# Twelve early tiles read two a batch, bias and tables moved, and a reordered drain in an attention and mixture-of-experts kernel

## The reference

```python
mod = (_silu(c) @ wmod).reshape(32, 6, 1, -1)
sa, ca, ga, sb, cb, gb = mod[:, 0] ... mod[:, 5]     # ga, gb: magnitude at least 0.25
h = _layernorm(x) * (1 + ca) + sa
...
x_proj = (h @ w_in.T + b_in).reshape(b, l, 16, -1); q, k, v = split(x_proj, 3)
att = softmax(einsum('blhd,bmhd->blmh', q, k) / sqrt(8), axis=2)
x = x + ga * (einsum('blmh,blhd->blhd', att, v).reshape(b, l, d) @ w_out.T + b_out)
h = _layernorm(x) * (1 + cb) + sb
...
logits = h @ router_w; assignments = argmax(logits); weights = softmax(logits)[assignments]
hid = gelu(einsum('nd,edf->nef', h, w1) + b1)        # 14 experts, 256 hidden
all_out = einsum('nef,efd->ned', hid, w2) + b2
x = x + gb * all_out[assignments] * weights
```

## Time and profile before

| | us |
|---|---|
| median of 3 runs | 638.29 (637.71 to 638.56) |
| the profiled execution's own time | 640.0 |
| its span on the core | 638.2 |
| busy: DVE | 557.4 (87%) |
| busy: ACT | 541.7 (85%) |
| busy: PE | 476.2 (75%) |
| busy: POOL | 476.6 (75%) |

### The profile page before, as it was taken

The page is one execution under the profiler, slowest core; times in us unless marked ns, Lnnn a source line. Parts: engine busy times, 40 slices in busy tenths (PEclk is TensorE's granted clock), DMA queues, the critical chain, the costliest instruction groups (busy, mean ns, idle before and its releaser), DMA issues.

```text
span 638.2 us, 11779 instructions
## 1 busy us (share of the span) xinstructions
PE 476.2 (75%) x2518; PEld 266.5 (42%) x2518; DVE 557.4 (87%) x1420; ACT 541.7 (85%) x2306; POOL 476.6 (75%) x661
## 2 busy tenths in 40 slices
PE   5446878877877877887878888876876679888870
PEld 3112334433333433343434333332432369778760
DVE  6977999999999999999999999997988768778770
ACT  1588999999999999999999999998999637666640
POOL 4453766888888888888887888867767857777774
PEclk9999965567566566556565565565555559999995
DMA  6355554545455555555454545556655124676740
GB/s 190 107 151 143 145 145 136 149 141 150 136 148 151 149 149 148 141 157 155 141 160 132 140 141 159 134 139 167 165 167 158 49 75 125 195 194 193 196 121 4
DMA packets 75416, 91.65 MB, mean 144 GB/s; under 512 B 12910, under 2 KB 59028, under 8 KB 75344
## 3 DMA queue, kind: packets, MB, share of 16 engines
q1 hardware_dynamic: 66810, 72.93, 42.4%
q0 software_dynamic: 6560, 16.83, 7.1%
q10 hardware_dynamic: 1976, 1.15, 0.7%
HBM read 58.41 MB, written 33.29 MB: 144 GB/s over the span
## 4 chain that ended last, share of the span: by engine, by line
ACT 42%; DVE 15%; DMA 10%; PE 8%; issue 8%; POOL 8%; SPq 8%; POOLq 0%; DVEq 0%; ACTq 0%
ACT scores L765 41%; DVE neg_max L1149 6%; SPq L481 6%; DMA x_s<-table 3%; DMA parts_dram<-parts 3%; DMA out_dram<-out_room,ids_s 2%; PE scores L1027 2%; POOL out_dram L743 2%; PE scores L1036 2%; POOL table L691 1%; DVE bn L1083 1%; POOL rstd L630 1%; SPq L557 1%; DMA out_dram<-out_room,x_s 1%; PE side_a L917 1%
## 5 line engine op out<-in xcount | busy, mean ns | idle before, releaser
L765 ACT ACTIVATE scores<-scores,neg_max 128x256 f32<-128x256 f32 x1024 | 466.1, 781 | 21.6 <-DVE neg_max L1149 21.2
L765 ACT ACTIVATION_READ_ACCUMULATOR scores<-scores,neg_max 128x1 f32 x1024 | 378.0, 542 | 0.0
L1149 DVE TENSOR_REDUCE neg_max<-scores 128x4 f32<-128x1024 f32 x256 | 308.9, 1210 | 5.8 <-PE scores L889 4.8
L889 PE MATMUL scores<-k_stack,q_stack 64*128 64x256 bf16 x1024 | 148.8, 391 | 83.0 <-ACT scores L765 72.2
L889 PEld LDWEIGHTS scores<-k_stack,q_stack 64*128 64x128 bf16 x1024 | 34.6, 106 | 168.4 <-ACT scores L765 122.4
L691 POOL DMA_INDIRECT table<-rows,place_i x64 | 65.8, 1028 | 30.3 <-issue 29.5
L743 POOL DMA_INDIRECT out_dram<-out_room,ids_s x61 | 62.3, 1022 | 18.6 <-issue 14.9
L799 ACT ACTIVATE hid<-scores,w_e 128x128 f32<-128x128 f32 x154 | 48.1, 364 | 15.8 <-PE scores L1027 15.4
L917 PE MATMUL side_a<-w_gated,opt_t 128*128 128x128 f32 x128 | 50.6, 499 | 0.0
L1027 PE MATMUL scores<-x_t,w_e 128*128 128x128 f32 x308 | 49.8, 286 | 0.1
L629 POOL TENSOR_TENSOR rstd<-mv,eps_s 128x4 f32<-128x4 f32 x37 | 7.4, 200 | 56.9 <-DVE mv L1114 41.4
(11 more groups left out here) (172 smaller groups left out, 874.6 us busy)
## 6 DMA issues: line engine op xcount, KB each, us to landing
x_s<-table SPq DMA_DIRECT2D x77, 192.5 KB, 2.6
q_stack<-parts_dram SPq DMA_DIRECT2D x192, 64.0 KB, 2.5
parts_dram<-parts SPq DMA_DIRECT2D x31, 384.0 KB, 2.7
k_stack<-parts_dram SPq DMA_DIRECT2D x186, 64.0 KB, 2.3
mod_b<-mod_rows SPq DMA_DIRECT2D x32, 256.0 KB, 3.8
x_s<-in_x_dram SPq DMA_DIRECT2D x13, 256.0 KB, 3.6
w1x_s<-in_w1x_dram SPq DMA_DIRECT2D x7, 258.0 KB, 2.9
w_s<-in_w_dram SPq DMA_DIRECT2D x7, 256.0 KB, 3.1
```

Of the source, the lines that this page charges most:

```text
L765: last = act.activation(buf[:, k * L:k * L + L], buf[:, k * L:k * L + L], ACT.Exp, bias=neg_max[:, p, n:n + 1], accum_out=exp_sum[:, p, n: ...
L889: last = pe.matmul(scores[:, c, at:at + L], q_stack[p][r, g + j, t * P:t * P + P], k_stack[p][r, g + j, :], start=True, stop=True)
L1149: dve.tensor_reduce(to, scores[:, (PAIRS * b.n + i) % RING, :].rearrange("p (e j m) -> p e j m", e=2, j=2), AX_X, ALU.max, negate=True).th ...
```

## The change

- **Early tiles.** `EARLY` 16 becomes 12, `EARLY_AT` 26 becomes 24 and `EARLY_STEP` 4 becomes 2: SP issues two row loads at the start of each of batches 24 to 29. The counts stand five to seven iterations ahead, in the batches 17 to 22 (`MAP_AT`); their result is stored in iteration 22 and read back in iteration 23, with no wait for the landing within one iteration. Tiles 12 to 76 need the map, 65 in place of 61, and `MAP_TURNED` goes from 9 to 7.
- **Batches 0 to 3.** `gated_bias_low` follows row_max 7 of batch 0. SP stores the bias in iteration 0, ahead of the parts, and loads it back after the first `load_mod`. `prepare_map` becomes three pieces, after row_max 4 of the batches 1, 2 and 3. In batch 1, `stats_x` of batch 4 follows row_max 1.
- **Every batch.** DVE does `invert_sums` ahead of `residual`.
- **Drain.** `weigh_rows` of the batches 29, 30 and 31 moves from POOL to DVE. POOL scatters the second tile of batch 28 in the drain. DVE loads all 12 experts at once, shifts h2 of batch 30 after that, fetches w1 four times in a row ahead of `residual(31)`, and does scale and shift of h2 of batch 31 ahead of the ranks' results. PE turns tiles 0 and 1 ahead of `turn_att`, and contracts tile 0 right after the last rank; ACT has the four copies early and the first two gelus right behind the table load. Until tile 7 the contraction lags by three tiles, not four; tiles 0 to 3 get bias, gate and sum at once. The PSUM buffers of the tile stage change places.

```diff
-EARLY = SLOTS
-EARLY_AT = 26
-EARLY_STEP = 4
+EARLY = 12
+EARLY_AT = 24
+EARLY_STEP = 2
+MAP_AT = EARLY_AT - 7
...
-MAP_TURNED = 9
+MAP_TURNED = 7
...
+                sp.wait_ge(x2_ready, -(-EARLY * ROW // (LT * D)))
                 for s in early_slots(b):
...
+                if b.n == EARLY_AT - 2:
                     sp.wait_ge(early_set, 1)
...
+                if b.n == EARLY_AT - 1:
                     sp.wait_ge(early_stored, 32)
...
                 load_late(b)
                 if b.n == 0:
                     sp.wait_ge(mod_ready, 1)
                     sp.dma_start(mod_rows, rows_out[:, :, :].rearrange("b r d -> b (r d)")).then_inc(mod_stored, 16)
+                    sp.wait_ge(bias_ready, 1)
+                    sp.dma_start(bias_dram.rearrange("r (b d) -> b r d", d=D), bias_out[:, :, :]).then_inc(bias_stored, 16)
                 else:
                     load_mod(b)
-                if b.n == 1:
-                    sp.wait_ge(bias_ready, 1)
-                    sp.dma_start(bias_dram.rearrange("r (b d) -> b r d", d=D), bias_out[:, :, :]).then_inc(bias_stored, 16)
-                    sp.wait_ge(bias_stored, 16)
-                    sp.dma_start(bias_rows[:, :, :].rearrange("r b d -> r (b d)"), bias_dram).then_inc(bias_loaded, 16)
...
                 if b.n == 0:
                     sp.wait_ge(mod_stored, 16)
                     load_mod(b)
+                    sp.wait_ge(bias_stored, 16)
+                    sp.dma_start(bias_rows[:, :, :].rearrange("r b d -> r (b d)"), bias_dram).then_inc(bias_loaded, 16)
...
-                pool.wait_ge(weighted, b.done())
+                if b.n < B - LATE:
+                    pool.wait_ge(weighted, b.done())
+                else:
+                    pool.wait_ge(weighted_late, b.n - (B - LATE) + 1)
                 steps.plain()
-                for t in range(LT):
+                for t in tiles:
                     pool.indirect_dma_start(table, bass.IndirectOffsetOnAxis(ap=place_i[g.n % RING_ROWS][:, at.start + t:at.start + t + 1], axis=0),
                                             rows[r][:, t, :], None).then_inc(scattered[r], 16)
...
                 last = Batch(B - 1)
                 attention_rows(last)
                 root(B + 4)
                 gate(last)
-                weigh_rows(last.ago(2))
-                scatter(last.ago(2))
+                scatter(last.ago(LATE), range(1, LT))
+                scatter(last.ago(2), range(LT))
                 root(B + 5)
-                weigh_rows(last.ago(1))
-                scatter(last.ago(1))
-                weigh_rows(last)
-                scatter(last)
+                scatter(last.ago(1), range(LT))
+                scatter(last, range(LT))
...
                 last = Batch(B - 1)
                 router_exp(group_of(B - 3))
+                copy_x(0)
+                copy_x(1)
                 take_att(last)
                 router_exp(group_of(B - 2))
-                gelu(0, 0, 0)
-                gelu(1, 1, 0)
+                copy_x(2)
+                copy_x(3)
                 router_exp(group_of(B - 1))
 
                 act.wait_ge(expl_ready, GROUPS)
                 act.activation(gelu_first[:, :], exp_l[:, 2 * LT - 1, 0:2], ACT.Gelu)
-
+                gelu(0)
+                gelu(1)
+
...
+                    expand(j - AT_W1)
+                if j < 2 * PRIMED:
+                    contract(j - AT_W2 + 1)
+                elif j > 2 * PRIMED:
+                    contract(j - AT_W2)
...
+                experts.extend(load_many(pe, expert_now, 0, EARLY, 0, E - 1))
+                pe.wait_ge(exped, PAIRS * B - 2)
+                turn_tile(0)
+                turn_tile(1)
                 turn_att(last)
                 project_v(last)
                 turn_h2(last.ago(1))
                 project_out(last)
                 route(last.ago(1))
-                tile(0, 0, 0)
-                tile(1, 1, 0)
+                turn_tile(2)
+                pe.wait_ge(exped, PAIRS * B)
+                expand(0)
+                expand(1)
                 rank(group_of(B - 2), B - 1)
-                tile(2, 2, 0)
+                turn_tile(3)
                 turn_h2(last)
                 route(last)
                 rank(group_of(B - 1), B)
-                tile(3, 3, 0)
+                contract(0)
...
+            def weigh_rows(b):
+
+                g = group_of(b.n)
+                r, at = b.slot(RING_ROWS), g.at(b.n)
+                dve.wait_ge(weighed, g.n + 1)
+                steps.plain()
+                steps.then(dve.tensor_scalar(rows[r][:, :, ID:ROW].bitcast(I32), token_id[:, :].rearrange("p (t o) -> p t o", o=1),
+                                             L * b.n + L, None, ALU.add))
+                dve.tensor_tensor(rows[r][:, :, GW:GW + D], mod_b[b.slot(RING_MOD)][:, MOD_GB:MOD_GB + 1, :].broadcast_to([P, LT, D]),
+                                  weight[g.n % 2][:, at].rearrange("p (t o) -> p t o", o=1).broadcast_to([P, LT, D]),
+                                  ALU.mult).then_inc(weighted_late, 1)
 
...
                 row_max(b, 1)
-                if norm.there():
-                    residual(norm)
+                if b.n == 1:
+                    stats_x(fresh)
                 if tail.there():
                     invert_sums(tail)
                 if norm.there():
+                    residual(norm)
                     stats_x2(norm)
...
-                if b.n == 1:
-                    gated_bias_low()
...
+                if b.n == 1:
+                    prepare_below()
+                if b.n == 2:
+                    prepare_map()
+                if b.n == 3:
+                    prepare_rows()
...
+                if b.n == 0:
+                    gated_bias_low()
...
-                if j == AT_W2:
+                n = j - AT_W2
+                if n < PRIMED:
+                    bias_y(n)
+                    gate_y(n)
+                    out_y(n)
+                    fetch_w1(j)
+                else:
+                    if in_range(n):
+                        bias_y(n)
+                    if in_range(j):
+                        fetch_w1(j)
+                    if in_range(n):
+                        gate_y(n)
+                    if n > PRIMED:
+                        out_y(n - 1)
+                if n == 0:
                     map_rows()
-                if j == AT_W2 + 1:
+                if n == 1:
                     map_columns()
...
-                dve.wait_ge(stats, B + 4)
-                steps.plain()
-                own_h2(norm, B + 4)
-                weigh_values(last)
-                take_h2(norm)
+                scale_h2(norm, B + 4)
                 dve.wait_ge(early_known, 32)
                 dve.wait_ge(w_moe_loaded, 16 * LOADS_MOE)
                 steps.plain()
-                load_experts(0, BUFS)
-                tile(0, 0, 0)
-                tile(1, 1, 0)
+                load_experts(0, EARLY)
+                shift_h2(norm, B + 4)
+                weigh_values(last)
+                take_h2(norm)
+                weigh_rows(last.ago(2))
+                for j in range(PRIMED):
+                    fetch_w1(j)
                 residual(last)
...
                 mark(one)
+                scale_h2(last, B + 5)
+                shift_h2(last, B + 5)
+                weigh(one)
+                invert_weight(one)
                 find_place(one)
                 count_rows(one)
                 own_place(one)
                 note_place(one)
-                weigh(one)
-                invert_weight(one)
-                dve.wait_ge(stats, B + 5)
-                steps.plain()
-                own_h2(last, B + 5)
-                tile(2, 2, 0)
-                tile(3, 3, 0)
                 take_h2(last)
-                load_experts(BUFS, SLOTS - BUFS)
+                weigh_rows(norm)
                 compare_last(last)
...
                 note_place(other)
+                weigh_rows(last)
                 map_counts()
```

215 lines of the change are left out of this document (113 added, 102 removed).

## The result

The changed kernel takes 633.95 us (median; 632.35 to 634.44) against 638.0 (637.36 to 638.56) for the kernel before: ratio 0.9933, 95% interval 0.9912 to 0.9953. It is 4 us faster, clear of the measurement, and a third of the forecast gain of 12.8; it lies outside the range of 620.5 to 632.0.

What follows compares the result with a forecast made beforehand. ACT's exponentials were taken to bound the middle batches and POOL's output scatters the tile stage. Terms 4.8 + 0 + 0.7 + 5.3 + 2.0 + 0 = 12.8 us off 638.3 gave 625.5, range 620.5 to 632.0.

Steps and rivals of the forecast that it cites:

- what is late next: Batches 0 to 3: bias_low done just before the parts' store; if late, about 1 us comes back.
- A: Batches 0 to 3: ACT's idle times at the start go; 4.8 us gained, bounds 3.5 and 5.3.
- F: Early counts moved from batches 20-25 to 17-22: same waits, no landing wait within an iteration; 0.7 us, bounds −0.5 and 1.8.
- B: Early loads, two a batch: half the bytes, half the delay in landing; 5.3 us gained, bounds 2.5 and 6.3.
- C: Drain after the last exponential: earlier shift and four tiles at once bring the sixth store earlier; 2.0 us, bounds −1.0 and 4.0.
- rival 2: Drain: DVE's three products each wait out a POOL operation of 1.04; C = −1.1, 628.6 us, chance 0.09.
- E: Every batch: inverting sums first fills residual's wait for PE, but ACT is saturated; 0 us.
- D: Tile stage: 77 scatters at 1.31 us unchanged, the map's loads hidden with 4 us to spare; 0 us.
- The three idle times: ACT's idle times in batches 0 to 2, 1.69, 0.62 and 2.56 us, together 4.87, all forecast to go.
- the 2.5 of slack: Batches with early loads: a delay of 4.5 gave 2.0 of stall, so some 2.5 us is absorbed; 2.3 just fits.
- rival 1: Early loads still stall, six batches having a bulk transfer ahead of the parts; B = 1.5, 629.3 us, chance 0.12.
- rival 5: Whole kernel: nothing comes of the change, since what is saved is waited for elsewhere; 638.3 us, chance 0.03.

Runs made afterwards that it cites:

- x5: The changed kernel with the early counts in batches 16 to 21, not 17 to 22; ratio 0.9925 to the kernel before.
- x8: The changed kernel with its twelve early loads as four in each of batches 26 to 28, counts still at 17; ratio 0.9955 to the kernel before.
- y1: The changed kernel with its fourteen expert weight loads two iterations earlier (10 to 23); ratio 0.9897 to the kernel before.
- x11: The changed kernel with counts at 16, the last nine pads in five stores, tile 4's bias, gate and sum at once; ratio 0.9908 to the kernel before.
- y2: The changed kernel with counts at 16, weights earlier, pad stores later, tile 4's sum at once, no contraction left out at step 8; ratio 0.9876 to the kernel before.

## Why the prediction was wrong

Three steps failed in mechanism or sign (what is late next in A, the constant price of the counts' waits in F, the landing in B that was to halve with the bytes), and one was sized too large (C, between the fourth and the sixth store). By its own terms, trace against trace:

| term | forecast | traces | |
|---|---|---|---|
| A, start | 4.8 | 5.2 gone, 1.7 to 3.2 back | failed: what is late next |
| E, swap | 0 | 0 in the total; about 1 of F's loss may be its | not settled |
| F, early counts | +0.7 | −3.0 | failed: sign |
| B, early loads | 5.3 | 4.0, in the repeats 3.1 and 3.8 | direction right; landing not halved |
| C, drain | 2.0 | 1.1 | right to the fourth store, then oversized |
| D, tile stage | 0 | 0 | right |

The changed kernel's three traces give 5.2 − 2.3 − 3.0 + 3.8 + 1.1 = 4.8 for the loop and drain together, with the middle values; the medians say 4.0.

**A.** The three idle times went as each step said, PE's wait for `bias_rows` too. The step that failed is the one that asked what is late next: I looked at DVE (bias_low) and at the parts' first store, and not at SP's whole iteration, the cover of which was ACT's own stall. A queue that is only just fast enough while the bound engine stalls becomes the bound when it doesn't.

**F.** "The same operations remain, so does what they wait out" was wrong. What they wait out hangs on which batch of a pair they stand in: 8.19 us for the seventeen operations in place of 6.82, three long waits in place of one. The other source, 1.3 of the 3.0, stays open (see x5). I had the row that showed such a wait, priced it as a constant, and looked only at how many iterations earlier the counts stood. The low bound of −0.5 had no row behind it: the row that could have given it is that 1.12, times the operations that it could befall. This term alone is 3.7 of the 8.8 that are missing.

**B.** Two loads a batch stall less than four (x8), but the step that sized it failed: half the bytes, half of the delay in landing, so stacks 4.1 after the parts' store, and under 4.5 as the sign. Of the six iterations one is under 4.5 (4.09 to 6.65). With an issue of 0.9 and a landing 2.0 over the plain 2.8, as in iteration 26, the delay is 2.9 by my estimate, not 2.3, and no longer fits into the 2.5 of slack. And 2.3 to 3.2 of stall stayed where I left 1.3 for the batches with weight loads; moving the weights away took about 1 of it (y1), by a way that isn't shown.

**C.** `compare_last` was forecast 0.8 earlier and came 1.1 earlier, the weigh_rows cost 0.43 and 0.16 (once 0.31) and met no POOL operation (rival 2 was wrong in its place; its mechanism turned up in the loop instead). By DVE's chain the fourth store was to come 25.9 behind the last exponential, and it did (25.86, by the measure of the earlier trace rows). The step that failed is "the sixth store comes two periods of 1.31 and some slack later": 2.9 were forecast and 3.8 passed. Tile 4's sum stands behind tile 5's bias, which waits 0.78 for PE (x11 frees the fifth store by its sum alone), and PE's left-out contraction holds the sixth (y2).

**D.** The store period is 1.330, not 1.312: sixth to seventy-seventh are 71 periods, and I divided by 72. Nothing hangs on it, since the change leaves the period as it is.

**The rivals and the range.** None of the five was the case: 633.95 lies between rival 1 (629.3) and rival 5 (638.3). Rival 1's row held in part, since the landing stayed near 5 behind two loads. Each rival took one term away; what happened was two fifths from A, all and more of F, and parts of B and C at once. The range had slips besides. The low bounds of the terms add up to 4.5 (3.5 − 0.5 + 2.5 − 1.0), not 7.5, and rivals 1 and 2 with A at its low end leave 4.6, not 6.3, which would have ended the range at 633.7. The measured gain of 4.0 lies just outside even that.
